# A graph layer with a routed feed-forward stage: three last tiles kept out of the sums, their rows gathered and matched in pairs, and the copy to the output in chunks of five rows

## The chip, the cores and the metric

One core of a Trainium2 chip runs the kernel. The metric is the time of the device in microseconds (us) of one execution. TensorE (PE in the profile, its weight loads PEld) multiplies matrices, VectorE (DVE) and ScalarE (ACT) work on elements, GpSimd (POOL) issues the indirect DMAs, SyncE (SP) and ScalarE issue the plain ones. All DMAs of the core run on its 16 DMA engines.

## What is computed

The input is x (1250 x 768) with a graph of 41250 edges. The kernel computes two graph attention layers and a linear attention, adds them to x, and then a routed feed-forward stage. Only this last stage matters here:

```python
gate = xt @ Wg + bg
scores, idx = jax.lax.top_k(gate, TOP_K)          # TOP_K = 2 of 8 experts
h = jax.nn.gelu(jnp.einsum('td,edh->eth', xt, W1) + b1[:, None, :], approximate=False)
y = jnp.einsum('eth,ehd->etd', h, W2) + b2[:, None, :]
comb = jnp.sum(jax.nn.one_hot(idx, NUM_EXPERTS, dtype=x.dtype) * scores[..., None], axis=1)
out = jnp.einsum('te,etd->td', comb, y)
x = x + out
```

So each row of the output is the row of x plus two weighted rows, one from each expert that was chosen for it.

## The kernel before, in words

The rows are sorted by expert into NTL = 27 tiles of 128 places. A tile holds rows of one expert only; places that are left over point at a row past the end (N = 1250 rows, NP = 1280). A row of x has two places, in two different tiles, because its two experts differ. `found[:, i]` holds, for each of the 128 places of tile i, the number of its row. `acc_d` in DRAM starts as x, and the weighted rows are added to it.

For each tile i, the following happens:

- Pool gathers the tile's normalized rows from `xf_d` into the buffer `XR[:, i % 3]` (`rows_gather`, line 863), three tiles ahead.
- TensorE turns them (`rows_in`, line 2183), ScalarE copies them out of PSUM (line 1113), TensorE multiplies by the first weights (`up`, products of line 1783 and a bias product of line 2192), ScalarE takes the Gelu (line 1118, for the last tile line 1121), TensorE turns the result (`turn`, line 2199), VectorE splits it into two fp16 parts (`HT`, lines 1756 and 1757), TensorE multiplies by the second weights (`down`, line 1783 and the bias product of line 2209), and VectorE scales the result by the score into `Yb[:, i % 2]` (line 1773).
- Pool adds `Yb` to the rows of `acc_d` by an indirect DMA that accumulates (`sums_add`, line 870). Each addition waits until the one before it has landed, since two tiles can hold the same row.

TensorE's order in the loop is: rows_in(i + 1), turn(i - 1), up(i), down(i - 1); behind the loop come turn(26), a product for shared rows, and down(26). VectorE's order is HT(i), then Yb(i). Each engine works through its own list in order, so what stands behind a waiting instruction waits too.

The last two tiles are not added to `acc_d`. LATE = NTL - 2 = 25 is the first of them. When the additions of tiles 0 to 24 have landed, `acc_d` is copied to `out`, rows 0 to 639 from SP's queue (line 749) and the other 610 from ACT's (line 1124), both as one contiguous block. At the same time Pool gathers the rows of tiles 25 and 26 from `acc_d` into XR (line 887). VectorE adds `Yb` of tile 25 to the first (line 1761). A row may stand in both tiles. The matrix `same` (128 x 128, one where place k of tile 25 and place n of tile 26 hold the same row) is made before the loop: TensorE spreads `foundf` of one tile over all partitions (line 2219), VectorE compares it with the other's (line 1745) and reduces it to a flag for each place (line 1747). A product of `same` with `Yb` of tile 25 (line 2238) is added to tile 26's rows (line 1765), and with its own result that gives the final rows (line 1770). Two scatters write them to `out` (lines 891 and 894), once both copies are complete; a place of tile 25 whose row stands in tile 26 too is skipped, because its number in `lasti` is made larger than N.

Of the kernel before, what the change touches and what calls it, by code (L numbers as in the profile page):

```python
# [15 lines left out]
P = 128  # L16
# [7 lines left out]
def gps_layer(nc, x, src, dst, norm_g, norm_b, W1, a_src1, a_dst1, b1, W2, a_src2, a_dst2, b2, Wu, bu,  # L24
# [27 lines left out]
    with ctx:  # L52
# [157 lines left out]
        def low(off, words, rows=P):  # L210
            return arena[0:rows, LOW + off:LOW + off + words]
# [67 lines left out]
        same = low(5 * D + MAPW, P)  # L279
        shared, lastf = low(5 * D + MAPW + P, 1), low(5 * D + MAPW + P + 1, 1)  # L280
        lasti = low(5 * D + MAPW + P + 2, 1).bitcast(I32)
        assert P + 3 <= MAPW
# [255 lines left out]
        LATE = NTL - 2  # L538
# [17 lines left out]
        def _(sp):  # L556
# [192 lines left out]
            sp.dma_start(out[0:NT // 2 * P, :], acc_d[0:NT // 2 * P, :]).then_inc(s_out_done, 16)  # L749
# [5 lines left out]
        def _(pool):  # L755
# [134 lines left out]
            pool.wait_ge(s_y_ready, NTL)  # L890
            g.indirect_dma_start(out=out, out_offset=bass.IndirectOffsetOnAxis(ap=lasti.bitcast(U32), axis=0), in_=XR[:, (LATE - 1) % 3, :], in_offset=None,
                                 bounds_check=N - 1, oob_is_err=False).then_inc(sums_out[LATE % 2], 16)
            pool.wait_ge(s_y_ready, NTL + 1)
            g.indirect_dma_start(out=out, out_offset=bass.IndirectOffsetOnAxis(ap=found[:, NTL - 1:NTL].bitcast(U32), axis=0), in_=Yb[:, (NTL - 1) % 2, :], in_offset=None,
                                 bounds_check=N - 1, oob_is_err=False).then_inc(sums_out[(NTL - 1) % 2], 16)
# [3 lines left out]
        def _(act):  # L899
# [209 lines left out]
            for i in range(NTL):  # L1109
# [16 lines left out]
        @block.vector  # L1126
        def _(dve):
# [620 lines left out]
            link(V.scalar_tensor_tensor(lastf, shared, float(4 * NP), foundf[:, LATE:LATE + 1], ALU.mult, ALU.add))  # L1748
            link(V.tensor_copy(lasti, lastf))

            for i in range(NTL):
# [6 lines left out]
                if i == NTL - 1:  # L1758
                    dve.wait_ge(s_y_ready, LATE + 1)
                    dve.wait_ge(rows_back[(LATE - 1) % 3], 16 * ((LATE - 1) // 3 + 2))  # L1760
                    V.tensor_tensor(XR[:, (LATE - 1) % 3, :], XR[:, (LATE - 1) % 3, :], Yb[:, LATE % 2, :], ALU.add).then_inc(s_y_ready, 1)
                    dve.wait_ge(s_same_psum, 1)
                    dve.wait_ge(rows_back[LATE % 3], 16 * (LATE // 3 + 2))
                    before = XR[:, LATE % 3, :].rearrange("p (a n) -> p a n", a=2)
                    link(V.tensor_tensor(before, PS[:, 0:1024].rearrange("p (a n) -> p a n", a=2)[:, :, 0:HALF], before, ALU.add))
                dve.wait_ge(s_y_psum, i + 1)
                if i >= 2:
                    dve.wait_ge(sums_out[i % 2], 16 * (i // 2))
                if i == NTL - 1:
                    V.scalar_tensor_tensor(Yb[:, i % 2, :].rearrange("p (a n) -> p a n", a=2), PS[:, 5 * 512:7 * 512].rearrange("p (a n) -> p a n", a=2)[:, :, 0:HALF],  # L1770
                                           score[:, 1, i:i + 1], before, ALU.mult, ALU.add).then_inc(s_y_ready, 1)
                    break
                V.tensor_scalar(Yb[:, i % 2, :].rearrange("p (a n) -> p a n", a=2), PS[:, 5 * 512:7 * 512].rearrange("p (a n) -> p a n", a=2)[:, :, 0:HALF], score[:, 1, i:i + 1], None, ALU.mult).then_inc(s_y_ready, 1)  # L1773

        @block.tensor
        def _(pe):
# [442 lines left out]
            T.matmul(ps[7][:, 0:P], foundf[:, NTL - 1:NTL].to_broadcast([P, P]), ident[:, :], start=True, stop=True).then_inc(s_map_psum, 1)  # L2219
# [15 lines left out]
            pe.wait_ge(s_y_ready, LATE + 1)  # L2235
# [31 lines left out]
```

## Time and profile before

| what | us |
|---|---|
| median of three runs | 1122.6 (1119.86 to 1125.56) |
| the profiled execution, its own time | 1124.17 |
| its span | 1122.4 |
| TensorE busy | 979.9 (87%) |
| VectorE busy | 763.9 (68%) |
| ScalarE busy | 332.1 (30%) |
| GpSimd busy | 117.8 (10%) |

Times within the trace are counted from the start of the span. "Busy" says that an engine had an instruction at work, not that it set the time. PEclk is the granted clock of TensorE as a share of full speed.
### The profile page before, as it was taken

How to read it: one execution, taken by the hardware profiler on the slowest of the kernel's cores; microseconds unless marked ns; L12 is line 12 of the kernel's file. 1: busy time of each engine (PE TensorE's matmuls, PEld its weight loads, DVE VectorE, ACT ScalarE, POOL GpSimd, SP SyncE). 2: the span in 40 equal slices, each digit the busy share in tenths (PEclk: the TensorE clock that was granted, in tenths of full speed). 3: DMA queues.
4: the chain of work that ended last, by engine and by line, in shares of the span. 5: the costliest groups of instructions: out<-in, count | busy, mean ns of one | idle time of the engine just before them, and what ended most of it. 6: DMA issues, size and time to landing. Idle time of an engine off the chain costs nothing.

```text
span 1122.4 us, 17272 instructions
## 1 busy us (share of the span) xinstructions
PE 979.9 (87%) x6464; PEld 707.8 (63%) x6466; DVE 763.9 (68%) x1711; ACT 332.1 (30%) x402; POOL 117.8 (10%) x125
## 2 busy tenths in 40 slices
PE   3699999999789989989988998959878399999992
PEld 2677776765454445546678998759765366666661
DVE  6576788878875686986587898499979823222321
ACT  3551122212004331422333343115335332222220
POOL 3000000000001000000000000000631123333321
PEclk9799999999989999999989999868898589999997
DMA  8341121144240926636686100006046545555535
GB/s 243 123 143 44 44 84 58 57 153 158 103 180 29 314 98 207 204 103 231 221 328 288 47 1 1 1 0 254 5 170 231 208 102 109 113 113 104 103 63 179
DMA packets 58570, 146.45 MB, mean 130 GB/s; under 512 B 11562, under 2 KB 30908, under 8 KB 55482
## 3 DMA queue, kind: packets, MB, share of 16 engines
q1 hardware_dynamic: 49482, 114.37, 28.9%
q0 software_dynamic: 6080, 21.24, 9.3%
q10 hardware_dynamic: 2928, 9.74, 2.3%
q8 instruction: 54, 0.88, 0.3%
q14 instruction: 26, 0.21, 0.1%
HBM read 96.73 MB, written 53.23 MB: 134 GB/s over the span
## 4 chain that ended last, share of the span: by engine, by line
PE 64%; DVE 21%; DMA 6%; issue 4%; ACT 3%; SPq 1%; DVEq 0%; POOLq 0%; ACTq 0%
PE PS L1783 37%; PE PS L2032 12%; PE PS L1859 3%; DVE arena L1522 3%; DVE arena L1478 2%; DVE arena L1484 2%; PE PS L2183 2%; DMA arena<-in_L_ffn_W_dram 1%; DMA arena<-acc_d,arena 1%; PE PS L1870 1%; DMA acc_d<-arena 1%; PE PS L1839 1%; PE PS L1874 1%; DVE arena L1494 1%; DVE arena L1384 1%
## 5 line engine op out<-in xcount | busy, mean ns | idle before, releaser
L1783 PE MATMUL PS<-arena 128*128 128x384 f16 (+7 forms) x3396 | 575.6, 323 | 5.5 <-DVE arena L1638 2.7
L1783 PEld LDWEIGHTS PS<-arena 128*128 128x128 f16 (+2 forms) x3396 | 321.6, 99 | 217.5 <-issue 12.8
L2032 PE MATMUL PS<-arena 128*128 128x193 f32 (+1 forms) x1200 | 190.5, 322 | 21.9 <-DVE arena L1484 16.6
L2032 PEld LDWEIGHTS PS<-arena 128*128 128x128 f32 x1200 | 186.0, 200 | 26.4 <-DVE arena L1484 16.1
L1046 ACT ACTIVATE arena<-arena,AS 128x1280 f32<-128x1280 f32 x60 | 81.8, 1363 | 132.4 <-DVE arena L1478 132.2
L1773 DVE TENSOR_SCALAR arena<-PS,arena 128x768 f32<-128x768 f32 x26 | 26.5, 1018 | 134.5 <-PE PS L2209 134.5
L1478 DVE SCALAR_TENSOR_TENSOR arena<-arena,AS 128x1280 f32<-128x1280 f32 x60 | 94.1, 1572 | 0.0
L1484 DVE SCALAR_TENSOR_TENSOR arena<-arena 128x1280 f32<-128x1280 f32 x60 | 90.5, 1508 | 3.5 <-PE PS L2032 3.5
L1286 DVE TENSOR_SCALAR arena<-arena 128x240 f16<-128x240 f16 x324 | 89.4, 276 | 0.0
L1285 DVE TENSOR_SCALAR arena<-arena 128x128 f16<-128x128 f16 x324 | 80.5, 248 | 0.1
L1113 ACT ACTIVATE arena<-PS 128x1536 f16<-128x1536 f16 x27 | 39.2, 1450 | 100.1 <-PE PS L2183 100.1
L1384 DVE CUSTOM_DVE_ANT_0 arena<-arena 128x1280 bf16<-128x1280 f32 x40 | 59.5, 1489 | 2.4 <-DMA arena<-as_d 1.6
L1859 PE MATMUL PS<-arena 128*128 128x240 f16 x324 | 44.8, 270 | 12.9 <-DVE arena L1278 12.9
L940 ACT ACTIVATE arena<-arena 128x768 f16<-128x768 f32 x48 | 39.8, 838 | 53.5 <-DMA arena<-in_L_ffn_W_dram 53.4
L1239 DVE SCALAR_TENSOR_TENSOR arena<-arena 128x768 f16<-128x768 f32 x48 | 45.5, 954 | 13.1 <-ACT arena L940 12.6
L870 POOL DMA_INDIRECT acc_d<-arena x25 | 39.7, 1586 | 118.6 <-DVE arena L1773 118.6
L1859 PEld LDWEIGHTS PS<-arena 128*128 128x128 f16 x324 | 31.1, 98 | 24.9 <-DVE arena L1286 15.6
L1278 DVE TENSOR_TENSOR arena<-arena,PS 128x240 f32 x81 | 32.4, 400 | 12.8 <-PE PS L1859 11.4
L863 POOL DMA_INDIRECT arena<-xf_d,arena x27 | 26.7, 988 | 63.8 <-DVE arena L1721 49.0
L1522 DVE CUSTOM_DVE_ANT_0 arena<-PS,arena 128x1280 bf16<-128x1280 f32 x20 | 28.4, 1485 | 5.4 <-PE PS L2048 5.4
L793 POOL MEMSET arena<- 128x768 bf16 x1 | 0.7, 743 | 288.3 <-DMA bias_d<-arena 288.3
L972 ACT ACTIVATE arena<-PS 128x384 f32<-128x384 f32 x20 | 8.7, 488 | 70.7 <-PE PS L1783 70.7
(289 smaller groups left out, 961.5 us busy)
## 6 DMA issues: line engine op xcount, KB each, us to landing
arena<-in_L_ffn_W_dram SPq DMA_DIRECT2D x48, 384.0 KB, 4.0
fr_d<-arena SPq DMA_DIRECT2D x48, 384.0 KB, 3.2
arena<-fr_d SPq DMA_DIRECT2D x16, 1152.0 KB, 14.4
arena<-in_x_dram SPq DMA_DIRECT2D x18, 384.0 KB, 5.3
arena<-rr_d SPq DMA_DIRECT2D x4, 1280.0 KB, 8.6
acc_d<-arena SPq DMA_DIRECT2D x11, 384.0 KB, 2.6
g_d<-arena SPq DMA_DIRECT2D x10, 388.0 KB, 2.4
acc_d<-arena ACTq DMA_DIRECT2D x10, 384.0 KB, 2.4
```

Of the source, the lines that this page charges most:

```text
L940: a.activation(cbuf[b][:, PIECE:PIECE + PIECE // 2].bitcast(F16), cbuf[b][:, 0:PIECE], ACT.Copy, scale=UP).then_inc(s_conv_high, 1)
L1046: a.activation(BUF[:, unit % 3, :], BUF[:, unit % 3, :], ACT.Exp, bias=AS2[:, h, t:t + 1]).then_inc(s_e_ready, 1)
L1239: V.scalar_tensor_tensor(buf[:, 0:PIECE // 2].bitcast(F16), buf[:, 0:PIECE], UP, buf[:, PIECE:PIECE + PIECE // 2].bitcast(F16), ALU.mult, ...
L1285: V.tensor_scalar(ohlo[:, u % OB, j, :], iota[:, 0:P], kc[:, 1, j, u:u + 1], None, ALU.is_equal)
L1286: i = V.tensor_scalar(ohk[:, u % OB, j, :], iota[:, 0:NT * W], kc[:, 0, j, u:u + 1], None, ALU.is_equal)
L1384: V.tensor_tensor_reduce(out=junk1, in0=arow1[h], in1=mask1[d % 2].rearrange("p t d -> p (t d)"), scale=1.0, scalar=-3e38, op0=ALU.subtrac ...
L1478: V.scalar_tensor_tensor(BUF[:, unit % 3, :], RR[:, h % 2, 0, :], AS8[:, h, t:t + 1], RR[:, h % 2, 1, :], ALU.add, ALU.max).then_inc(s_t2_ ...
L1484: V.scalar_tensor_tensor(PT[i % deep], BUF[:, unit % 3, :], 2.0, CT[:, t, 0:NP], ALU.min, ALU.mult).then_inc(s_p_ready, 1)
L1522: V.tensor_tensor_reduce(out=junk2[:, n % 2, :], in0=PS[:, bank:bank + NP], in1=mask2[:, t, :], scale=1.0, scalar=-3e38, op0=ALU.subtract, ...
L1783: m = T.matmul(out, left[i][x], right[i][y], start=first and i + r == 0, stop=last and 3 * i + r == n - 1)
L1859: i = T.matmul(ps[4 + u % 2][:, 0:NT * W], ohlo[:, u % OB, j, :], ohk[:, u % OB, j, :], start=j == 0, stop=j == EJ - 1)
L2032: m = T.matmul(ps[b][:, r * (C + 1):(r + 1) * (C + 1)], PT[i % deep][:, d * P:(d + 1) * P], feats, start=t == 0 and r == 0, stop=t == NT - ...
```

## The change

LATE becomes NTL - 3 = 24, so tiles 24, 25 and 26 are kept out of the sums. Their rows are gathered from `acc_d`, each tile into the XR buffer that its own rows have left. A row can now stand in two of the three tiles, in three ways, so `same` becomes three matrices (24 in 25, 24 in 26, 25 in 26), and TensorE makes three products behind turn(26) instead of one. `shared` and `lasti` have two columns. VectorE adds Yb(24) to tile 24's gathered rows directly behind Yb(24) in its order. The copy of `acc_d` to `out` is cut at row 650 instead of 640, and both parts are named as ten times 13 (or 12) chunks of five rows of 3072 bytes, with the ten outermost. ACT's copy now stands ahead of its last Gelu. Three scatters follow the copies instead of two. The core of the diff:

```diff
-        LATE = NTL - 2
+        LATE = NTL - 3
+        CUT = 650
@@ SP
-            sp.dma_start(out[0:NT // 2 * P, :], acc_d[0:NT // 2 * P, :]).then_inc(s_out_done, 16)
+            sp.dma_start(out[0:CUT, :].rearrange("(a b r) n -> b a (r n)", b=10, r=5), acc_d[0:CUT, :].rearrange("(a b r) n -> b a (r n)", b=10, r=5)).then_inc(s_out_done, 16)
@@ Pool
             for i in range(LATE, NTL):
-                b = (i - 1) % 3
-                pool.wait_ge(s_xrt_psum, i)
+                b = i % 3
+                pool.wait_ge(s_xrt_psum, i + 1)
                 g.indirect_dma_start(out=XR[:, b, :], out_offset=None, in_=acc_d,
...
+            for i in range(LATE, NTL):
+                pool.wait_ge(s_y_ready, (LATE + 2, LATE + 4, LATE + 5)[i - LATE])
+                last = i == NTL - 1
+                g.indirect_dma_start(out=out, out_offset=bass.IndirectOffsetOnAxis(ap=(found[:, i:i + 1] if last else lasti[:, i - LATE:i - LATE + 1]).bitcast(U32), axis=0),
+                                     in_=Yb[:, i % 2, :] if last else XR[:, i % 3, :], in_offset=None,
+                                     bounds_check=N - 1, oob_is_err=False).then_inc(sums_out[i % 2], 16)
@@ ScalarE, in the tile loop
+                if i == NTL - 1:
+                    for b in range(2):
+                        act.wait_ge(sums_out[b], added(b, LATE))
+                    a.dma_start(out[CUT:N, :].rearrange("(a b r) n -> b a (r n)", b=10, r=5), acc_d[CUT:N, :].rearrange("(a b r) n -> b a (r n)", b=10, r=5)).then_inc(s_out_done, 16)
...
-            for b in range(2):
-                act.wait_ge(sums_out[b], added(b, LATE))
-            a.dma_start(out[NT // 2 * P:N, :], acc_d[NT // 2 * P:N, :]).then_inc(s_out_done, 16)
@@ VectorE, before the tile loop
-            V.tensor_scalar(same, ps[7][:, 0:P], foundf[:, LATE:LATE + 1], None, ALU.is_equal).then_inc(s_found_ready, 1)
+            for k, (a, b) in enumerate(((0, 1), (0, 2), (1, 2))):
+                j = V.tensor_scalar(same[:, k, :], ps[7][:, (b - 1) * P:b * P], foundf[:, LATE + a:LATE + a + 1], None, ALU.is_equal)
...
-            link(V.tensor_reduce(shared, same, axis=AX.X, op=ALU.max))
+            V.tensor_reduce(shared[:, 0:1], same[:, 0:2, :].rearrange("p k n -> p (k n)"), axis=AX.X, op=ALU.max)
+            link(V.tensor_reduce(shared[:, 1:2], same[:, 2, :], axis=AX.X, op=ALU.max))
+            def rows_read(i):
+                dve.wait_ge(rows_back[i % 3], 16 * (i // 3 + 2))
+
+            def shared_add(i, banks):
+                for c in range(2):
+                    h = rows_of(i)[:, c * HALF:(c + 1) * HALF]
+                    k = V.tensor_tensor(h, h, ps[banks[c]][:, 0:HALF], ALU.add)
+                link(k)
@@ VectorE, behind HT(NTL - 1)
+                    rows_read(LATE + 1)
                     dve.wait_ge(s_same_psum, 1)
+                    shared_add(LATE + 1, (0, 1))
+                    V.tensor_tensor(rows_of(LATE + 1), rows_of(LATE + 1), Yb[:, (LATE + 1) % 2, :], ALU.add).then_inc(s_y_ready, 1)
+                    rows_read(LATE + 2)
+                    dve.wait_ge(s_same_psum, 2)
+                    shared_add(LATE + 2, (7, 3))
@@ VectorE, behind Yb(i)
+                if i == LATE:
+                    dve.wait_ge(s_y_ready, LATE + 1)
+                    rows_read(LATE)
+                    V.tensor_tensor(rows_of(LATE), rows_of(LATE), Yb[:, LATE % 2, :], ALU.add).then_inc(s_y_ready, 1)
+                elif i == LATE + 1:
+                    dve.wait_ge(s_y_ready, LATE + 3)
@@ TensorE
-                    pe.wait_ge(s_y_ready, i)
+                    pe.wait_ge(s_y_ready, i + max(0, i - LATE - 1))
...
-            T.matmul(ps[7][:, 0:P], foundf[:, NTL - 1:NTL].to_broadcast([P, P]), ident[:, :], start=True, stop=True).then_inc(s_map_psum, 1)
+            for b in range(2):
+                m = T.matmul(ps[7][:, b * P:(b + 1) * P], foundf[:, LATE + 1 + b:LATE + 2 + b].to_broadcast([P, P]), ident[:, :], start=True, stop=True, skip_group_check=True)
+            m.then_inc(s_map_psum, 1)
...
-            for c in range(2):
-                m = T.matmul(ps[c][:, 0:HALF], same, Yb[:, LATE % 2, c * HALF:(c + 1) * HALF], start=True, stop=True)
-            m.then_inc(s_same_psum, 1)
+            def shared_part(k, y, banks, first, last):
+                for c in range(2):
+                    m = T.matmul(ps[banks[c]][:, 0:HALF], same[:, k, :], Yb[:, y % 2, c * HALF:(c + 1) * HALF], start=first, stop=last)
+                return m
+
+            shared_part(0, LATE, (0, 1), True, True).then_inc(s_same_psum, 1)
+            shared_part(1, LATE, (7, 3), True, False)
+            pe.wait_ge(s_y_ready, LATE + 3)
+            shared_part(2, LATE + 1, (7, 3), False, True).then_inc(s_same_psum, 1)
             down(NTL - 1, before)
```

## Rows read from the trace of the kernel before

**Rows 1.** The chain that ended last, 1080 to 1123 us: start, us, what

```profile
1084.53 7.09 DMA acc_d<-arena
...
1092.34 5.37 DMA acc_d<-arena
...
1097.98 14.69 DMA arena<-acc_d,arena
```

**Rows 2.** Timeline, 1060 to 1123: start, us, engine, line, what [idle before <-releaser]

```profile
1093.64 0.33 PE L2192 MATMUL PS<-arena 104*128 104x384 bf16 x1
...
1094.00 0.49 ACT L1121 ACTIVATE arena<-PS 128x384 f32<-128x384 f32 x1 [6.19 <-PE PS L2192]
...
1097.06 0.49 PE L2199 MATMUL PS<-ident,arena 128*128 128x128 f32 x3
1097.26 1.02 DVE L1773 TENSOR_SCALAR arena<-PS,arena 128x768 f32<-128x768 f32 x1 [4.60 <-PE PS L2209]
1097.73 0.61 SPq L749 DMA_DIRECT2D out_dram<-acc_d  x1
...
1098.34 1.56 PE L2238 MATMUL PS<-arena 128*128 128x384 f32 x4 [0.78 <-DVE arena L1773]
1098.78 0.56 DVE L1757 TENSOR_TENSOR arena<-PS,arena 128x384 f16<-128x384 f32 x1
1099.30 0.98 POOL L887 DMA_INDIRECT arena<-acc_d,arena  x1 [0.31 <-issue]
...
1099.73 1.63 PE L1783 MATMUL PS<-arena 128*128 x9
...
1102.82 0.33 PE L2209 MATMUL PS<-arena 104*128 104x384 bf16 x1
1112.76 0.96 DVE L1761 TENSOR_TENSOR arena<-arena 128x768 f32<-128x768 f32 x1 [13.42 <-DMA arena<-acc_d,arena]
...
1114.68 1.02 DVE L1770 SCALAR_TENSOR_TENSOR arena<-PS,arena 128x768 f32<-128x768 f32 x1
1116.53 1.01 POOL L894 DMA_INDIRECT out_dram<-arena  x1 [0.87 <-DVE arena L1770]
```

**Rows 3.** DMA queues, stretches 1099:1101.7, 1101.7:1104.35, 1104.35:1105.4: packets, MB, share

```profile
q1 hardware_dynamic: 16, 0.98, 102.1%
...
q10 hardware_dynamic: 16, 0.94, 96.7%
...
q1 hardware_dynamic: 16, 0.98, 282.7%
q0 software_dynamic: 16, 0.10, 28.5%
```

**Rows 4.** Timeline at the start of the tile loop, 885 to 918

```profile
902.08 0.80 PE L2219 MATMUL PS<-ident,arena 128*128 128x128 f32 x2
...
907.83 0.56 DVE L1756 CAST arena<-PS 128x384 f16<-128x384 f32 x1 [3.78 <-PE PS L2199]
```

**Rows 5.** DMA view of 1084 to 1092, in 40 slices of 0.2 us

```profile
GB/s 0 0 0 0 0 0 0 0 0 0 0 0 0 230 15 108 154 108 138 61 61 200 215 200 215 123 108 97 15 0 0 0 0 0 0 0 0 0 0 0
```

**Rows 6.** DMA queues, 576 to 581, loads of 1152 KB: packets, MB, share

```profile
q1 hardware_dynamic: 133, 2.02, 96.4%
```

**Rows 7.** DMA view, 788 to 793: six loads of eight rows

```profile
DMA packets 97, 0.12 MB, mean 24 GB/s; under 512 B 48, under 2 KB 72, under 8 KB 96
```

**Rows 8.** Line 863, the row gathers of the tile loop

```profile
DMA to landing us min/median/max: 4.0/5.1/5.9
```

**Rows 9.** Stretches (start:end us): busy us (instructions) of each engine, PEclk, DMA, GB/s

```profile
309.00:316.60 7.60, 6.74 (x24) 3.40 (x25) 3.40 (x18) 0.00 (x0) 0.00 (x0) 0.50 1.02 378
572.60:576.04 3.44, 3.42 (x11) 3.44 (x12) 3.44 (x3) 1.36 (x1) 0.12 (x1) 0.50 0.51 148
1103.20:1108.50 5.30, 0.00 (x0) 0.00 (x0) 0.00 (x0) 0.00 (x0) 0.00 (x0) 1.00 1.16 370
1108.50:1112.00 3.50, 0.00 (x0) 0.00 (x0) 0.00 (x0) 0.00 (x0) 0.00 (x0) 0.50 0.38 134
```

More of the change, by code:

```diff
@@ L278, in gps_layer @@
         foundf = low(5 * D, NTL)
[L279 to L282, printed above, removed]
+        same = v3(low(5 * D + MAPW, 3 * P), 3)
+        shared, lastf = (low(5 * D + MAPW + 3 * P + 2 * k, 2) for k in range(2))
+        lasti = low(5 * D + MAPW + 3 * P + 4, 2).bitcast(I32)
+        assert MAPW + 3 * P + 6 <= D
         found = small(NTL).bitcast(I32)
@@ L536, in copies_of @@
             return range(s - 4, s - 3) if s < NT + 2 else range(2 * s - NT - 6, 2 * s - NT - 4)
-        LATE = NTL - 2
+        LATE = NTL - 3
+        CUT = 650
+        assert CUT < N and CUT % 50 == 0 and (N - CUT) % 50 == 0
         def added(b, n):
@@ L889, in _ @@
             pool.wait_ge(s_out_done, 32)
[L890 to L895, printed above, removed]
+            for i in range(LATE, NTL):
[4 more added lines that the diff above has]
+                                     bounds_check=N - 1, oob_is_err=False).then_inc(sums_out[i % 2], 16)
         @block.scalar
@@ L1744, in _, with rows_of @@
             dve.wait_ge(s_map_psum, 3)
-            V.tensor_scalar(same, ps[7][:, 0:P], foundf[:, LATE:LATE + 1], None, ALU.is_equal).then_inc(s_found_ready, 1)
+            for k, (a, b) in enumerate(((0, 1), (0, 2), (1, 2))):
+                j = V.tensor_scalar(same[:, k, :], ps[7][:, (b - 1) * P:b * P], foundf[:, LATE + a:LATE + a + 1], None, ALU.is_equal)
+            j.then_inc(s_found_ready, 1)
             dve.wait_ge(s_found_ready, 3)
-            link(V.tensor_reduce(shared, same, axis=AX.X, op=ALU.max))
-            link(V.scalar_tensor_tensor(lastf, shared, float(4 * NP), foundf[:, LATE:LATE + 1], ALU.mult, ALU.add))
+            V.tensor_reduce(shared[:, 0:1], same[:, 0:2, :].rearrange("p k n -> p (k n)"), axis=AX.X, op=ALU.max)
+            link(V.tensor_reduce(shared[:, 1:2], same[:, 2, :], axis=AX.X, op=ALU.max))
+            link(V.scalar_tensor_tensor(lastf, shared, float(4 * NP), foundf[:, LATE:LATE + 2], ALU.mult, ALU.add))
             link(V.tensor_copy(lasti, lastf))
+            def rows_of(i):
+                return XR[:, i % 3, :]
+            def rows_read(i):
[5 more added lines that the diff above has]
+                link(k)
             for i in range(NTL):
@@ L1758, in _ @@
                 if i == NTL - 1:
-                    dve.wait_ge(s_y_ready, LATE + 1)
-                    dve.wait_ge(rows_back[(LATE - 1) % 3], 16 * ((LATE - 1) // 3 + 2))
-                    V.tensor_tensor(XR[:, (LATE - 1) % 3, :], XR[:, (LATE - 1) % 3, :], Yb[:, LATE % 2, :], ALU.add).then_inc(s_y_ready, 1)
+                    rows_read(LATE + 1)
                     dve.wait_ge(s_same_psum, 1)
-                    dve.wait_ge(rows_back[LATE % 3], 16 * (LATE // 3 + 2))
-                    before = XR[:, LATE % 3, :].rearrange("p (a n) -> p a n", a=2)
-                    link(V.tensor_tensor(before, PS[:, 0:1024].rearrange("p (a n) -> p a n", a=2)[:, :, 0:HALF], before, ALU.add))
+                    shared_add(LATE + 1, (0, 1))
[3 more added lines that the diff above has]
+                    shared_add(LATE + 2, (7, 3))
                 dve.wait_ge(s_y_psum, i + 1)
                 if i >= 2:
-                    dve.wait_ge(sums_out[i % 2], 16 * (i // 2))
+                    dve.wait_ge(sums_out[i % 2], 16 * (min(i, LATE) // 2 if i % 2 == 0 else min(i // 2, LATE // 2)))
                 if i == NTL - 1:
+                    dve.wait_ge(s_same_psum, 2)
+                if i == NTL - 1:
+                    before = rows_of(i).rearrange("p (a n) -> p a n", a=2)
                     V.scalar_tensor_tensor(Yb[:, i % 2, :].rearrange("p (a n) -> p a n", a=2), PS[:, 5 * 512:7 * 512].rearrange("p (a n) -> p a n", a=2)[:, :, 0:HALF],
```

1 line of the change is left out of this document (removed).

## The prediction, made before the change was run

> **What bounds the kernel now.** I read the chain that ended last first, then the timeline of the last 60 us, then the DMA view of the same stretch in short slices. The tile loop is bound by TensorE up to tile 26, the last. The end is bound by transfers. The chain [rows 1] shows the addition of tile 23's rows to acc_d (issued at 1084.53, landed 7.09 us later, at 1091.6), that of tile 24 (issued at 1092.34, landed at 1097.71), and then 14.69 us for the gather of tile 25's rows back from acc_d, to 1112.67. TensorE has finished long before: its last matmul begins at 1102.82 and takes 0.33, so it ends at 1103.15 [rows 2]. Then VectorE runs from 1112.76 to 1115.70, and the last scatter is issued at 1116.53 [rows 2]. So the two gathers and the two copies of acc_d to out, all issued from 1097.73 to 1099.30 [rows 2], set the end.
>
> Why does a gather take 14.7 us, when the loop's gathers land 5.1 us after their issue [rows 8]? The three slices of the DMA view [rows 3] show it. From 1099 to 1101.7 there are 16 packets of SP's queue and nothing else, from 1101.7 to 1104.35 16 of ACT's queue, and then 16 of the gathers' (q0) before the next 16 of SP's. Each of the 16 DMA engines thus takes one packet of each queue in turn. A copy's packet is 0.98 MB / 16 = 61 KB and takes 102.1% x 16 x 2.7 us / 16 = 2.76 us (22 KB/us); a gather's is 0.10 MB / 16 = 6 KB, two rows, and takes 28.5% x 1.05 us = 0.30 us. A gather of 128 rows has four of them per engine, then an end marker.
>
> **The change, part by part.** I follow tile 24's rows, which after the change are gathered, and no longer added to acc_d.
>
> 1. Start of the copies. They now wait for tile 23's sum alone, landed at 1091.6 instead of 1097.71: 6.1 us earlier [rows 1]. SP's queue is otherwise empty. On ACT the copy now stands ahead of the last Gelu, which starts at 1094.00 [rows 2]; the issue begins at about 1091.7 and takes about the 0.61 us of SP's [rows 2], so 1.7 us of slack cover it. Without that cover the Gelu would be late by as much, but turn(26), which reads it, comes only after the new wait of step 3. Pool's gathers go from two to three, each 1.3 us after the one before (0.98 and 0.31 idle [rows 2]): at about 1091.9, 1093.2 and 1094.5.
>
> 2. Landing of gather 24. Its first data move about 2.1 us after the issue (tile 23's sum: issued at 1084.53, first slice with data at 1086.6 [rows 1, 5]), so at 1094.0. The copies' first packets start 1.4 us after the issue (issued at 1097.73, and all 16 of SP's first packets lie in the slice that begins at 1099 and fill it, [rows 2, 3]), so at 1093.05. Their chunks are five rows, 15.4 KB. No row before shows such a copy between two DRAM tensors. The lower bound is a load of packets of 15 KB, 96.4% x 16 x 5 / 133 = 0.58 us [rows 6]; the upper one is 0.75 us, the rate of the later 61 KB packets (282.7% x 1.05 = 2.97 us [rows 3]). I take 0.69, from 2.76 us for 61 KB, the same kind of transfer at its first, less mixed packets. One turn is 0.69 + 0.69 + 0.27 = 1.65 us. The first gather packet goes at 1093.05 + 2 x 0.69 = 1094.4, the marker four turns on at 1101.0, and the gather lands at 1101.2. The bounds are 1097.0 (5.1 us after the issue, [rows 8]) and 1103.3 (0.9 us a packet, if small packets carry a cost of their own).
>
> 3. What waits for it. VectorE's add for tile 24 is put between Yb(24) and the HT copies of tile 25. So the wait for the gather now stands ahead of those copies, and TensorE's down(25) waits for them. In the kernel before these went on at 1098. TensorE ends up(26) at 1093.97 [rows 2] and idles. From the landing on, everything runs in series: the add 0.96 (1.05 with its start), HT(25) 1.1 (from 1098.28 to 1099.34), down(25) 3.8 (1099.34 to 1103.15), turn(26) 0.5, three shared parts of 1.4 each (L2238: 1098.34 to 1099.73 for one, and there are now three) 4.2, down(26) 3.4 (1099.73 to 1103.15), and the last VectorE instruction 1.05: in sum 15.1 us [rows 2]. HT(26), and the new adds for tiles 25 and 26 (five instructions of 0.56 to 1.0), run beside the shared parts and down(26), and Yb(25) ends before part three needs it. That gives 1101.2 + 15.1 = 1116.3 as the end of VectorE, against 1115.70 before.
>
> 4. The clock. TensorE idles from 1093.97 to about 1103.4, 9.4 us. Before, it had the full granted clock for 5.3 us of idling and half of it (1.2 instead of 2.4 GHz) from 1108.5 on [rows 9]. So down(25) starts at half. When work came back after such gaps, the clock stayed at half for 3.4 us in one case (572.60 to 576.04) and 7.6 us in another (309.00 to 316.60) [rows 9]. The mean is 5.5 us, and half of it is lost: 2.7 us (1.7 to 3.8). VectorE then ends at 1119.0, or 3.3 us later than before.
>
> 5. Setup of the matches. Two fp32 products stand before the loop instead of one. One shows as two records, 0.80 us in all [rows 4]; TensorE starts the loop right behind them, so the second costs at most 0.8 and, since the two are pipelined, about 0.3. The added VectorE work (two comparisons, a wider reduction) is under 1.5 us and lies inside the 3.78 us that VectorE idles before its first HT copy [rows 4]. I take 0.3.
>
> 6. The transfers' own end. Each of the six loads of eight rows left eight end markers (48 packets under 512 B [rows 7]): a queue's transfer uses as many engines as its outer count allows. With an outer count of ten the copies run on ten engines, 13 and 12 chunks on each: 1093.05 + 25 x 0.69 + 12 x 0.27 = 1113.5, about as late as before in spite of the earlier start. The other two gathers end within a us of that. Pool then issues three scatters at 1.3 us each: the third could go at 1116.4, while step 4 asks for 1119.8. So the transfers are late second, not first.
>
> The sum: 3.3 + 0.3 = +3.6 us. The profiled execution took 1124.17 with a span of 1122.4, and would become 1127.8; it lies 1.6 above the median of the three runs, so the median becomes 1122.6 + 3.6 = 1126.2.
>
> **The rivals.**
>
> - Gather 24 lands unhindered, at 1097.0, and TensorE's gap of 5.3 us doesn't lower the clock. VectorE would end at 1112.1, but the transfers hold: with 0.58 us a packet the copies end at 1110.7, the last gather at about 1111.3, and its two VectorE instructions at 1113.4. That is 2.3 less, 0.3 more for the setup: -2.0, 1120.6. For it: q0 is served in turn and its packets are short. Against it: in rows 3 the turns are strict.
> - The copies' packets cost 0.9 us, and the ten engines decide. Gather 24 lands at 1103.3, the copies end at 1093.05 + 22.5 + 3.2 = 1118.8 and the third scatter goes at 1121.7 instead of 1116.53: +5.2 + 0.3, 1128.1. It decides from about 0.85 us a packet.
> - Slower still: a queue's turn holds several chunks. If it held all 13, gather 24 would wait for both copies: 1093.05 + 25 x 0.69 + 4 x 0.27 + 0.2 = 1111.6, 10.4 later than in the forecast, 1136.6. Against it: the loads of rows 6 leave one packet per 15 KB row. The Trainium skill (DMA: Bandwidth & Descriptors, Queues, rings and completion order) says that an engine drains a whole packet, typically 9 to 17 descriptors, from one ring before it goes to the next; by that rule this rival is the forecast. The trace doesn't show such packets on SP's queue.
> - The clock stays at half to the end of the chain: the 11.5 us of TensorE's work in step 3 double. Above the 2.7 taken that is +8.8, 1135.0. Against it: the chain keeps TensorE busy after its resumption, and in both cases of rows 9 the clock came back.
>
> **How the numbers follow.** The forecast 0.60, unhindered 0.12, ten engines 0.12, several chunks a turn 0.08, half clock 0.08. Within 0.5% (5.6 us, about what a measurement of this kernel can tell from no change) lie nearly all of the first two and half of the third: 0.70. Slower by more are the last two, the other half of the third and a tail of the first: 0.25. To be faster by 5.6 us VectorE would have to end at 1110.1, earlier than gather 24's lower bound allows: 0.05. The range takes in the unhindered case with 2 us to spare and ten engines with 3: 1118.5 to 1131.5, leaving out the two at 1135 and later.
>
> **What would show it.** In the profile after: two HT copies of tile 25 that start near 1102 with a wait of some 10 us before the VectorE add; TensorE idle for about 9 us after up(26), a granted clock of 0.5 behind that; 25 packets of 15 KB on ten engines only; the last VectorE instruction at about 1119. The prediction is wrong if gather 24 lands before 1099 or after 1104, if the clock holds, or if the last scatter waits for the copies.

## The result and the profile after

The changed kernel takes 1127.9 us (median of seven runs) against 1122.6: a ratio of 1.0045, with a 95% interval of 1.003 to 1.006. Timed once more beside the kernel before, it came out at 1.0022 (1.0003 to 1.0041). So it is slower by a quarter to a half of a percent, 2.5 to 5 us. The forecast was +3.6 us, 1126.2. The profiled execution has a span of 1126.1 us; the forecast was 1126.0. That agreement to 0.1 us is luck: a second profile of the same kernel has a span of 1123.6.

The chain that ended last in the changed kernel, 1080 to 1127 us (start, us, what):

```profile
1092.24 10.94 DMA arena<-acc_d,arena
...
1104.73 0.57 DVE arena L1775
...
1105.43 3.06 PE PS L1810 x9
...
1111.11 3.87 PE PS L2268 x12
```

One gather sets it off, as in [rows 1], but it takes 10.94 us and is followed by TensorE's work, which in the kernel before was over by then. The timeline shows the same stretch (start, us, engine, line, what, idle before and its releaser):

```profile
1091.53 0.89 SPq L751 DMA_DIRECT2D out_dram<-acc_d  x1
1091.54 1.71 ACTq L1124 DMA_DIRECT2D out_dram<-acc_d  x1
1091.69 1.02 DVE L1794 TENSOR_SCALAR arena<-PS,arena 128x768 f32<-128x768 f32 x1 [5.20 <-PE PS L2236]
...
1092.24 1.02 POOL L889 DMA_INDIRECT arena<-acc_d,arena  x1 [5.05 <-issue]
...
1094.75 0.33 PE L2219 MATMUL PS<-arena 104*128 104x384 bf16 x1
...
1095.11 0.49 ACT L1127 ACTIVATE arena<-PS 128x384 f32<-128x384 f32 x1 [6.19 <-PE PS L2219]
1103.27 0.96 DVE L1798 TENSOR_TENSOR arena<-arena 128x768 f32<-128x768 f32 x1 [10.56 <-DMA arena<-acc_d,arena]
...
1105.43 3.06 PE L1810 MATMUL PS<-arena 128*128 x9 [10.36 <-DVE arena L1775]
...
1110.94 4.04 PE L2268 MATMUL PS<-arena 128*128 128x384 f32 x12
...
1118.34 1.02 DVE L1791 SCALAR_TENSOR_TENSOR arena<-PS,arena 128x768 f32<-128x768 f32 x1 [2.23 <-issue]
1120.15 0.98 POOL L895 DMA_INDIRECT out_dram<-arena  x1 [3.38 <-DVE arena L1791]
```

Up(26) ends at 1095.08. VectorE waits 10.56 us for the gather of tile 24, the two HT copies of tile 25 stand behind that wait (the second ends at 1105.29), and TensorE idles for 10.36 us. All else follows in series up to 1119.36. In [rows 2] up(26) ended at 1093.97 and down(25) followed at once.

The granted clock over the gap and behind it (start:end, length, busy us with the count of instructions for PE, PEld, DVE, ACT, POOL, then PEclk, DMA share, GB/s):

```profile
1095.10:1099.00 3.90, 0.00 (x0) 0.00 (x0) 0.00 (x0) 0.49 (x1) 0.70 (x1) 1.00 0.93 364
1099.00:1105.40 6.40, 0.00 (x0) 0.00 (x0) 1.98 (x3) 0.00 (x0) 0.00 (x0) 0.51 0.63 267
1105.43:1109.40 3.97, 3.97 (x13) 1.97 (x14) 0.00 (x0) 0.00 (x0) 0.00 (x0) 0.50 0.62 261
1109.40:1114.00 4.60, 4.60 (x22) 2.92 (x20) 3.08 (x6) 0.00 (x0) 1.02 (x1) 1.00 0.19 81
```

And the DMA queues over the copies (1092.8 to 1112.3), one turn of the engines (1103.6 to 1105), the stretch in which the copies begin (1092.8 to 1095.4), and the slice with the first packets of ACT's queue (1096.4 to 1096.6): packets, MB, share.

```profile
q1 hardware_dynamic: 140, 2.00, 25.3%
q10 hardware_dynamic: 130, 1.84, 22.3%
q0 software_dynamic: 240, 1.18, 15.9%
...
q1 hardware_dynamic: 10, 0.15, 25.6%
q10 hardware_dynamic: 10, 0.15, 25.6%
q0 software_dynamic: 10, 0.06, 10.4%
...
q1 hardware_dynamic: 34, 0.52, 57.0%
...
q10 hardware_dynamic: 5, 0.08, 104.0%
```

In the first three rows, 130 and 120 chunks of 15.4 KB are counted, with ten end markers for each of the two copies. One turn, 1103.6 to 1105, holds ten packets of each queue: ten engines, on each one packet of SP, one of ACT, one of the gathers. 25.6% x 16 x 1.4 / 10 = 0.573 us is a chunk's time, 0.233 a gather packet's. From 1092.8 to 1095.4 only SP's queue moves anything, 34 chunks: neither ACT's copy, issued at 1091.54, nor the first gather, issued at 1092.24, had begun. The gathers' first packets come at 1095.4, 3.2 us behind the issue, and ACT's at 1096.4, 4.9 us behind its own. So the turns of one packet for each queue are there later, but not at the start.

**How the runs are compared.** The part ahead of the tail varies from one execution to the next: Yb(24), the scaling of tile 24 on VectorE, starts anywhere from 1085.9 to 1093.9 us in the profiles of this study, though nothing ahead of it differs but the setup of the matches. So each profile is also read from the start of Yb(24) to the end of the span. It is called the tail below. Part of the tail still varies by chance: the sum of tile 23, behind which the copies and gathers of the changed kernels start, lands anywhere from 0.4 us before Yb(24)'s start to 1.1 us after it. So the table also gives the time from that landing to the end (SP issues its copy 0.06 us behind the landing, and that is where the landing is read in the kernels with three late tiles). The profiles are single executions; only the ratios come with an interval.

| kernel | Yb(24) starts | span | tail | from tile 23's landing | ratio to before (95%) |
|---|---|---|---|---|---|
| before | 1090.59 | 1122.4 | 31.8 | 30.8 | |
| changed | 1091.69 | 1126.1 | 34.4 | 34.6 | 1.0045 (1.003 to 1.006) |
| e13_changed_again | 1088.90 | 1123.6 | 34.7 | 34.5 | 1.0022 (1.0003 to 1.0041) |
| e1_add_later | 1090.69 | 1119.5 | 28.8 | 29.2 | 0.9977 (0.9958 to 0.9996) |
| e2_add_later_16 | 1088.49 | 1115.4 | 26.9 | 27.0 | 0.9970 (0.9948 to 0.9992) |
| e11_add_later_whole | 1089.16 | 1117.1 | 27.9 | 27.6 | 0.9949 (0.9925 to 0.9973) |
| e9_two_rows_16 | 1093.89 | 1120.2 | 26.3 | 26.1 | 0.9931 (0.9908 to 0.9954) |
| e12_two_rows_again | 1089.70 | 1115.8 | 26.1 | 26.3 | 0.9944 (0.9919 to 0.9969) |
| e4_sixteen | 1090.41 | 1128.2 | 37.8 | 36.7 | 1.0048 (1.0025 to 1.0072) |
| e3_whole_copies | 1091.59 | 1129.5 | 37.9 | 38.1 | 1.0063 (1.0040 to 1.0086) |
| e8_before_16 | 1085.94 | 1118.0 | 32.1 | 31.1 | 0.9993 (0.9972 to 1.0014) |
| e5_no_copies | 1087.81 | 1115.9 | 28.1 | 27.2 | one execution |
| e6_filler | 1090.70 | 1124.9 | 34.2 | 34.5 | one execution |
| e10_filler_60 | 1089.73 | 1122.4 | 32.7 | 33.1 | one execution |

### The profile page after: what moved, and what is told of

Read it like the earlier page. It is cut to its first block and busy times, and to the rows that moved or that the text cites. A ratio compares the mean times of both kernels' runs of the same rounds, so it can differ in the third digit from the quotient of the medians.

```text
span 1126.1 us, 17301 instructions
## 1 busy us (share of the span) xinstructions
PE 985.7 (88%) x6474; PEld 713.3 (63%) x6476; DVE 767.7 (68%) x1718; ACT 332.6 (30%) x402; POOL 118.3 (11%) x126
## 5 line engine op out<-in xcount | busy, mean ns | idle before, releaser
L2059 PE MATMUL PS<-arena 128*128 128x193 f32 (+1 forms) x1200 | 193.4, 325 | 21.9 <-DVE arena L1487 16.5
L2059 PEld LDWEIGHTS PS<-arena 128*128 128x128 f32 x1200 | 188.9, 202 | 26.3 <-DVE arena L1487 16.0
L872 POOL DMA_INDIRECT acc_d<-arena x24 | 38.1, 1588 | 112.4 <-DVE arena L1794 112.4
```

The source lines that it names most:

```text
L2059: m = T.matmul(ps[b][:, r * (C + 1):(r + 1) * (C + 1)], PT[i % deep][:, d * P:(d + 1) * P], feats, start=t == 0 and r == 0, stop=t == NT - ...
```

## The experiments

Theory A is the forecast's: VectorE's wait for gather 24 stands ahead of the HT copies of tile 25, TensorE stops, and the serial chain behind the landing sets the end. Theory B is the rival that the transfers set it, with the copies on ten engines.

### The add moved behind HT(26)

```diff
@@ VectorE, behind HT(NTL - 1)
+                    dve.wait_ge(s_y_ready, LATE + 2)
+                    rows_read(LATE)
+                    V.tensor_tensor(rows_of(LATE), rows_of(LATE), Yb[:, LATE % 2, :], ALU.add).then_inc(s_y_ready, 1)
                     rows_read(LATE + 1)
@@ VectorE, behind Yb(i)
-                if i == LATE:
-                    dve.wait_ge(s_y_ready, LATE + 1)
-                    rows_read(LATE)
-                    V.tensor_tensor(rows_of(LATE), rows_of(LATE), Yb[:, LATE % 2, :], ALU.add).then_inc(s_y_ready, 1)
-                elif i == LATE + 1:
-                    dve.wait_ge(s_y_ready, LATE + 3)
```

The counts that TensorE and Pool wait for are changed to match.

> The changed kernel with VectorE's add for tile 24 moved behind HT(26), so that no HT copy stands behind the wait for gather 24. Theory A (the wait in VectorE's order stops TensorE, and the serial chain behind it sets the end): TensorE no longer idles for 10 us, down(26) ends at 1095.1 + 3.3 + 0.5 + 4.2 + 3.4 = 1106.5, then the transfers decide: last gather 1112.1, two VectorE instructions of 1.0, end of VectorE 1114.2 instead of 1119.4, so about -5 us against the changed kernel: 1122.8, level with the kernel before. Theory B (the copies on ten engines set the end): nothing moves, 1127.9 within 1 us.

The timeline of e1_add_later:

```profile
1093.91 1.63 PE L1807 MATMUL PS<-arena 128*128 x9
...
1102.35 0.96 DVE L1779 TENSOR_TENSOR arena<-arena 128x768 f32<-128x768 f32 x1 [2.90 <-DMA arena<-acc_d,arena]
...
1104.46 0.33 PE L2233 MATMUL PS<-arena 104*128 104x384 bf16 x1
1108.42 1.02 DVE L1766 TENSOR_TENSOR arena<-arena,PS 128x384 f32<-128x384 f32 x2 [5.12 <-DMA arena<-acc_d,arena]
...
1111.56 1.02 DVE L1794 SCALAR_TENSOR_TENSOR arena<-PS,arena 128x768 f32<-128x768 f32 x1
...
1113.51 0.98 POOL L895 DMA_INDIRECT out_dram<-arena  x1 [0.31 <-issue]
```

TensorE goes on at once (1093.91) and ends at 1104.79, with the last matmul's record at 1104.46. The wait for gather 24 is still there, 2.90 us in front of the add at 1102.35, and costs nothing. What is late now is gather 25 (5.12 us of waiting before 1108.42), gather 26 and the copies, after which the three scatters go out 1.3 us apart, the last at 1113.51. The tail fell from 34.4 to 28.8, by 5.6 us where A expected 5 and B nothing. The ratio fell from 1.0045 to 0.9977; A had expected only to come level with the kernel before. One moved wait is the whole of the loss and more: A holds. B is right about what comes second, as step 6 had it.

### The copies on 16 engines, with the add moved and without

```diff
-            sp.dma_start(out[0:CUT, :].rearrange("(a b r) n -> b a (r n)", b=10, r=5), acc_d[0:CUT, :].rearrange("(a b r) n -> b a (r n)", b=10, r=5)).then_inc(s_out_done, 16)
+            sp.dma_start(out[0:640, :].rearrange("(a b r) n -> b a (r n)", b=16, r=5), acc_d[0:640, :].rearrange("(a b r) n -> b a (r n)", b=16, r=5)).then_inc(s_out_done, 16)
+            sp.dma_start(out[1200:N, :].rearrange("(a b r) n -> b a (r n)", b=10, r=5), acc_d[1200:N, :].rearrange("(a b r) n -> b a (r n)", b=10, r=5)).then_inc(s_out_done, 16)
```

ACT copies rows 640 to 1199 in the same way. e2_add_later_16 has this and the moved add, e4_sixteen this alone.

> As e1_add_later, and the copies with 16 outermost instead of ten (rows 0 to 639 and 640 to 1199 in chunks of five rows, the last 50 rows apart). Theory A: both limits move. Copies 15 packets of 0.57 and 12 gather packets of 0.23 on each engine, 11.4 us from 1093.2 on, so the last gather lands near 1106, TensorE ends near 1106.5, VectorE near 1108: -11 us against the changed kernel, 1116.5, about 0.5% faster than before. Theory B expects the gain of the copies alone: about -5.

> The changed kernel with only the copies spread over 16 engines, the chunks still five rows, VectorE's order untouched. Theory A: a gather packet still waits for one packet of each copy queue in every turn, gather 24 lands at about 1103 as before, and the chain behind it is unchanged: 1127.9 within 1.5. Theory B: copies end near 1106 instead of 1111.6: -5 us, 1123.

The gathers and the last VectorE instruction in e2_add_later_16, then the wait for gather 24 in e4_sixteen:

```profile
1088.43 0.65 SPq L751 DMA_DIRECT2D out_dram<-acc_d  x1
...
1102.30 0.96 DVE L1780 TENSOR_TENSOR arena<-arena 128x768 f32<-128x768 f32 x1 [5.06 <-DMA arena<-acc_d,arena]
1104.63 1.02 DVE L1767 TENSOR_TENSOR arena<-arena,PS 128x384 f32<-128x384 f32 x2 [1.36 <-DMA arena<-acc_d,arena]
...
1107.60 1.02 DVE L1795 SCALAR_TENSOR_TENSOR arena<-PS,arena 128x768 f32<-128x768 f32 x1
1109.42 0.98 POOL L896 DMA_INDIRECT out_dram<-arena  x1 [0.94 <-DVE arena L1795]
...
1105.33 0.96 DVE L1799 TENSOR_TENSOR arena<-arena 128x768 f32<-128x768 f32 x1 [13.89 <-DMA arena<-acc_d,arena]
```

With the add moved, the 16 engines bring the tail down to 26.9, 7.5 us less than in the changed kernel where 11 had been expected. The direction is A's; the size was wrong in two places. Gather 25 landed 16.2 us behind SP's issue and gather 26 about 17, where 14.5 had been expected for the last, because I added packet times as if 16 engines ran at the pace of ten: in e4_sixteen, over 1092.5 to 1107, SP's queue has a share of 43.2% of 14.5 us for 138 chunks, 0.73 us each, where the same reading gave 0.61 on ten. And VectorE ended 4.0 us behind gather 25's landing, where 2 had been allowed behind the last gather's.

Without the moved add, 16 engines gained nothing, as A said, and B's -5 us did not come. But gather 24 did not land as before, as A had it: it took 12.92 us from its issue instead of 10.94. The add waited 13.89 us instead of 10.56, and the tail grew by 3.4, to 37.8. Of that, 1.4 us is chance: in this execution the sum of tile 23 landed 1.1 us behind the start of Yb(24), in the changed kernel's 0.2 us before it. Counted from the landing the end is 2.0 us later, as much as gather 24 is. The ratio, 1.0048, can't be told from the changed kernel's. In this order, then, ten engines did no harm: their copies end at 1111.6, 7.8 us before VectorE, so their slower end costs nothing, and gather 24 comes 2.0 us sooner.

### The whole copies

e3_whole_copies is the changed kernel with the contiguous halves of the kernel before, e11_add_later_whole that with the moved add.

```diff
-            sp.dma_start(out[0:CUT, :].rearrange("(a b r) n -> b a (r n)", b=10, r=5), acc_d[0:CUT, :].rearrange("(a b r) n -> b a (r n)", b=10, r=5)).then_inc(s_out_done, 16)
+            sp.dma_start(out[0:NT // 2 * P, :], acc_d[0:NT // 2 * P, :]).then_inc(s_out_done, 16)
```

> The changed kernel with the copies of the kernel before (contiguous halves, packets of 61 and 58 KB on 16 engines). Theory A: gather 24 has to sit through both packets of each copy queue on every engine and lands at about 1106.3 instead of 1103.2, the chain starts 3 us later: 1131. Theory B: the copies end 5 us earlier than with ten engines, 1123.

> The changed kernel with VectorE's add moved as in e1_add_later, and the whole, contiguous copies of the kernel before. If chunks matter only through the number of engines: transfers end some 17 us after the copies' issue as with five-row chunks on 16 engines, and the end of the span is 27 us behind Yb(24)'s start, as in e2_add_later_16. If small packets help by themselves, it is 2 us or more later than that.

The VectorE add that waits for gather 24, in the one and in the other, then gather 24 from issue to landing in e4_sixteen and in e3_whole_copies (start, us, what):

```profile
1106.79 0.96 DVE L1798 TENSOR_TENSOR arena<-arena 128x768 f32<-128x768 f32 x1 [14.19 <-DMA arena<-acc_d,arena]
...
1105.43 0.96 DVE L1779 TENSOR_TENSOR arena<-arena 128x768 f32<-128x768 f32 x1 [7.52 <-DMA arena<-acc_d,arena]
...
1092.32 12.92 DMA arena<-acc_d,arena
...
1092.16 14.54 DMA arena<-acc_d,arena
```

In e3_whole_copies the add starts at 1106.79, 3.5 us later than in the changed kernel, and the tail is longer by 3.5. The edit undoes two things at once, the chunks and the ten engines, and e4_sixteen stands between them. From issue to landing, gather 24 took 10.94 us with five-row chunks on ten engines, 12.92 with the same chunks on 16, and 14.54 with whole halves on 16. So in these profiles 2.0 us of the 3.6 go with the ten engines and 1.6 with the chunks. Both matter because a chain hangs on this landing. B expected a gain from the 16 engines and none came. With the add moved, the same late landing costs little: tail 27.9, 1.0 more than with chunks on 16 engines, 0.9 less than with chunks on ten. There gathers land together and late, and five VectorE instructions and the final one follow in series.

### The copies nearly left out

e5_no_copies copies 16 rows on each queue instead of 650 and 600. Most rows of its output are never written.

```diff
-            sp.dma_start(out[0:CUT, :].rearrange(...), acc_d[0:CUT, :].rearrange(...)).then_inc(s_out_done, 16)
+            sp.dma_start(out[0:16, :], acc_d[0:16, :]).then_inc(s_out_done, 16)
```

> The changed kernel with the two copies of acc_d to out cut down to 16 rows each, so most rows of the output are never written. It prices the contention. Theory A: gather 24 lands about 5 us after its issue instead of 10.9, TensorE idles for some 5 us instead of 10.4, and the chain behind the landing keeps its length of about 15 to 16 us: end of VectorE 5 to 6 us earlier against Yb(24) than in the changed kernel. Theory B (transfers) expects gather 24 and the end to move by the same amount too; the two differ in what is left: by A the end is still 15 to 16 us behind gather 24's landing though no transfer is under way any more, by B VectorE ends right behind the last gather, at about 1100.

```profile
1089.46 1.02 POOL L889 DMA_INDIRECT arena<-acc_d,arena  x1 [6.15 <-issue]
...
1093.43 0.96 DVE L1798 TENSOR_TENSOR arena<-arena 128x768 f32<-128x768 f32 x1 [4.59 <-DMA arena<-acc_d,arena]
...
1108.10 1.02 DVE L1791 SCALAR_TENSOR_TENSOR arena<-PS,arena 128x768 f32<-128x768 f32 x1 [2.23 <-issue]
```

In the DMA view, from 1090.4 to 1090.8 and from 1090.8 to 1091.2:

```profile
q10 hardware_dynamic: 32, 0.05, 42.1%
...
q0 software_dynamic: 4, 0.02, 47.1%
```

Gather 24 landed 3.9 us after its issue, where A expected 5, so the copies cost it 7 us. Part of that is a late start. Here ACT's copy, issued at 1088.76, moves its data between 1090.4 and 1090.8, and the gathers begin between 1090.8 and 1091.2, under 2 us behind the issue of 1089.46. In the changed kernel the same two waited 4.9 and 3.2 us. So the late start there goes with SP's large copy under way, and is no fixed delay of the two queues; by what mechanism no run shows. The last VectorE instruction still ends 15.8 us behind the landing (1093.33 to 1109.12), with no copy or gather under way for the last 12. That is A, and B is out: with the transfers gone, the chain alone gives a tail of 28.1 us, more than e2_add_later_16 has with full copies. VectorE's end came 6.4 us earlier against Yb(24) than in the changed kernel, where 5 to 6 had been expected.

### The clock

Matmuls whose result nobody reads fill TensorE's gap.

```diff
                 up(i, e)
+                if i == NTL - 1:
+                    for _ in range(48):
+                        T.matmul(ps[7][:, 0:HALF], identh[:, :], XRTP[:, 0, 0, 0:3, :].rearrange("p k n -> p (k n)"), start=True, stop=True)
                 if i:
                     down(i - 1, before)
```

> The changed kernel with 48 matmuls of 384 columns, whose result nobody reads, between up(26) and down(25), about 7.8 us of TensorE work in the gap. Theory of the clock: the granted clock stays at full, down(25) takes 3.4 instead of 5.35 us, and the chain from gather 24's landing to the end of VectorE shrinks from 16.2 to about 14.3 us. If the clock had no part in it, the chain stays at 16.2.

> As e6_filler, but 60 matmuls instead of 48, 9.9 us, so that no more than about 0.6 us of idling is left ahead of down(25) (with 48, TensorE idled for 2.55 us and the granted clock was at half for 3.4 us all the same). If the clock has its part in the chain, it stays at full and the chain from gather 24's landing to the end of VectorE takes about 14.3 us instead of 16.2. If not, it stays near 16.

The stretches of e6_filler (48) and then of e10_filler_60 (60), columns as above:

```profile
1101.88:1104.43 2.55, 0.00 (x1) 0.00 (x1) 1.98 (x3) 0.00 (x0) 0.00 (x0) 1.00 0.65 277
...
1105.00:1108.40 3.40, 3.40 (x13) 1.54 (x12) 0.00 (x0) 0.00 (x0) 0.00 (x0) 0.50 0.57 236
...
1102.86:1103.60 0.74, 0.00 (x1) 0.00 (x1) 0.57 (x2) 0.00 (x0) 0.00 (x0) 1.00 0.68 291
1103.61:1107.00 3.39, 3.39 (x22) 2.16 (x23) 0.00 (x0) 0.00 (x0) 0.00 (x0) 1.00 0.63 261
```

With 48, the filler ended 2.55 us before down(25) could start, and the clock still went to half from 1105.0 to 1108.4: a miss, and no answer to the question (its chain took 16.0 us). With 60, the gap was 0.74 us and the clock held. The chain from the landing (1101.36) to the end of VectorE (1115.62) then took 14.3 us, as expected, against 16.2 in the changed kernel (1103.18 to 1119.36). The clock's part is 1.9 us, and the tail fell by 1.7, to 32.7. Each of the two is one execution.

### The kernel before with chunked copies

e8_before_16 is the kernel before with only its copies changed, in the chunks of e2_add_later_16.

```diff
-            sp.dma_start(out[0:NT // 2 * P, :], acc_d[0:NT // 2 * P, :]).then_inc(s_out_done, 16)
+            sp.dma_start(out[0:640, :].rearrange("(a b r) n -> b a (r n)", b=16, r=5), acc_d[0:640, :].rearrange("(a b r) n -> b a (r n)", b=16, r=5)).then_inc(s_out_done, 16)
```

> The kernel before (two late tiles) with only its copies changed: chunks of five rows on 16 engines, the last 50 rows apart. Theory A, by which small packets by themselves give nothing once the copies and the gathers end together: the last gather lands within 1 us of before, 1122.7 within 1.5. If small packets free the gathers: both land some 2 to 3 us earlier, 1120.

0.9993 (0.9972 to 1.0014), tail 32.1 against 31.8: nothing. Where copies and gathers all have to be in before the end, the size of the copies' packets didn't matter here.

### Chunks of two rows

e9_two_rows_16 is e2_add_later_16 with r=2 and the last 34 rows as one block on SP's queue; e12_two_rows_again is the same kernel.

```diff
-            sp.dma_start(out[0:640, :].rearrange("(a b r) n -> b a (r n)", b=16, r=5), ...)
-            sp.dma_start(out[1200:N, :].rearrange("(a b r) n -> b a (r n)", b=10, r=5), ...)
+            sp.dma_start(out[0:640, :].rearrange("(a b r) n -> b a (r n)", b=16, r=2), ...)
+            sp.dma_start(out[1216:N, :], acc_d[1216:N, :]).then_inc(s_out_done, 16)
```

> As e2_add_later_16, but with chunks of two rows (6 KB) instead of five, the last 34 rows as one block. A turn of an engine costs 0.23 x 3 = 0.7 us instead of 1.4, so the gathers come through before the copies end: gather 26 lands before the copies, VectorE ends near TensorE, and the third scatter follows the copies' end by 0.3 + 2.6: about 2 us less against Yb(24) than e2_add_later_16 (26.9 from there to the end of the span, so 25). If small packets cost more per byte, the copies end later and nothing is gained.

> The kernel of e9_two_rows_16 once more, timed beside e11_add_later_whole and the kernel before: about 0.5 to 0.7% faster than before, and 26 to 27 us from Yb(24)'s start to the end of the span. If the first measurement was a chance of the chip, it is level with e2_add_later_16, 0.3% faster.

The first five lines are of e12_two_rows_again, with its first scatter among them, the last is the add for tile 24 in e9_two_rows_16:

```profile
1099.57 0.96 DVE L1780 TENSOR_TENSOR arena<-arena 128x768 f32<-128x768 f32 x1 [1.12 <-DMA arena<-acc_d,arena]
...
1106.18 1.02 DVE L1767 TENSOR_TENSOR arena<-arena,PS 128x384 f32<-128x384 f32 x2 [0.34 <-DMA arena<-acc_d,arena]
1107.24 1.02 DVE L1795 SCALAR_TENSOR_TENSOR arena<-PS,arena 128x768 f32<-128x768 f32 x1
1107.24 1.02 POOL L896 DMA_INDIRECT out_dram<-arena  x1 [13.43 <-DMA out_dram<-acc_d]
...
1109.88 0.98 POOL L896 DMA_INDIRECT out_dram<-arena  x1 [0.30 <-issue]
...
1104.84 0.96 DVE L1780 TENSOR_TENSOR arena<-arena 128x768 f32<-128x768 f32 x1 [2.19 <-DMA arena<-acc_d,arena]
```

The add for tile 24 starts 9.9 us behind the start of Yb(24) in e12_two_rows_again and 11.0 in e9_two_rows_16, where it was 11.7 in e1_add_later and 13.8 in e2_add_later_16, and the three gathers now come one after the other. The first scatter follows the copies' end, and the other two follow it without a gap, the last 1.6 us behind VectorE's end at 1108.26. The tails are 26.3 and 26.1 where 25 had been expected: the copies ended 15.8 and 16.1 us behind their issue, against 15.1 with five rows in e2_add_later_16, which takes back 0.7 to 1.0 of the 2 us. Against e2 the two-row chunks gain 0.6 to 0.8 us of tail, which the ratios can't resolve. Against the kernel before, 0.9931 and 0.9944 are clear: this kernel, three late tiles with the add behind HT(26), is about 0.6% faster than the kernel before and about 1% faster than the changed one.

### The changed kernel once more

> The changed kernel itself once more. In its first profile the end of the span was 34.4 us behind the start of Yb(24), against 31.8 before, so the changed part accounts for +2.6 us, while the medians differ by 5.3. If the rest lies in the part ahead of Yb(24), which the change doesn't touch, and is a matter of the runs, the ratio comes out nearer to 1.0025 and the tail again near 34.4. If the tail itself varies and the first profile had a short one, the tail comes out at 36 to 37 and the ratio near 1.0045.

The tail was 34.7 and the ratio 1.0022: the first of the two. The changed part accounts for +2.6 and +2.9 us of tail in the two profiles. Counted from the landing of tile 23's sum it is +3.8 and +3.7: in the profile before that sum took 7.09 us to land, in these two 5.8 and 6.2, which makes their tails look shorter. The rest of the first timing's +5.3 isn't explained by anything behind the landing; the two intervals meet at 1.003 to 1.0041, and I take +3.4 to +4.6 us as what both allow.

## Why the prediction was right, step by step

The size came out right, but in part because two misses cancel each other. Counted from the landing of tile 23's sum (1091.6 before, 1091.47 after):

- **Step 1, start of the copies: right.** SP issued at 1091.53 and ACT at 1091.54. ACT's issue took 1.71 us instead of the 0.61 assumed; its Gelu started at 1095.11, so the cover held, and it held with 1.9 us left. The gathers followed at 1092.24, 1093.57 and 1094.85, the first 0.8 us behind the landing and not 0.3.
- **Step 2, landing of gather 24: the turns right, the start wrong.** Forecast 9.6 us behind the sum, measured 11.7 (1103.18). Strict turns of one packet for each queue are there, and on ten engines, but only once all three queues move. A turn cost 1.4 us, not 1.65, since a chunk took 0.573 us, the lower bound of [rows 6] and not the 0.69 that I took from the 61 KB packets. The start was the error: I let gather data begin 2.1 us after the issue [rows 5] and take turns with both copies from then on, and nothing of q0 moved before 1095.4, 3.2 us after it, while SP's queue alone moved 34 chunks. Four turns of 1.4 us back from the end marker, 0.2 us ahead of the landing, the first gather packet on the ten shared engines came at about 1097.4 (an estimate), some 3 us later than my 1094.4. The shorter turns give 1.0 back, and +2.1 us is left. e5_no_copies shows that the 2.1 us were not too short for a gather without large copies beside it.
- **Step 3, the serial chain: right, 0.8 us too long.** 14.3 us at full clock (e10_filler_60) against 15.1. The add and the first HT copy overlap by 0.1, and the three shared parts took 3.9 us to the next matmul and not 4.2.
- **Step 4, the clock: right, 0.8 us too large.** It was at half from 1099 to 1109.4, 4.0 us of them behind down(25)'s start, and cost 1.9 us, inside the bounds of 1.7 to 3.8. Its two cases in [rows 9], 3.4 and 7.6 us, were averaged to 5.5; the shorter was nearer. The second miss, 1.6 us in steps 3 and 4 together, stands against the 2.1 of step 2.
- **Step 5, the setup: right.** The two products began at 903.29 and the loop's first at 904.30, 1.0 us after it where it was 0.9 before: 0.1 instead of 0.3. VectorE idled 2.40 us ahead of its first HT copy instead of 3.78.
- **Step 6, the transfers second: right.** Copies ended at 1111.6, forecast 1113.5; the first scatter went at 1112.46 and the third waited 3.38 us for VectorE, not for the copies. e1_add_later shows them take over once the chain is gone.

Of the rivals, the unhindered gather fell in step 2: it was e5_no_copies that had it, at the price of no copies. Ten engines as the bound, several chunks a turn, and a clock at half to the end didn't occur. (The last has a slip: TensorE's work in step 3 adds up to 11.9 us, not 11.5, and the rival to 1135.4; nothing else hangs on it.) The rule of the Trainium skill (DMA: Bandwidth & Descriptors, Queues, rings and completion order) by which a turn holds 9 to 17 descriptors would have put the landing at 1111.6; the landing was at 1103.18, and the turns of the profile after hold one 15 KB chunk of each queue. Before the other queues moved, SP's sent over three chunks an engine.

What the prediction did not look for is that the +3.6 us were avoidable: it priced the wait where it stood. The diff already shows that the add for tile 24 writes rows that only the first scatter reads, so HT(25), Yb(25) and HT(26) can all go ahead of it.

## What to carry to other kernels

- When work is taken out of a DMA queue and given to a compute engine, find what stands behind its wait in that engine's order before looking at the transfer. Here one wait placed ahead of two copies turned a gain of 3.0 us of tail into a loss of 2.6 (1.6 and 3.8 counted from the landing of tile 23's sum); placed five instructions later it cost nothing.
- Chunking a large copy brings a small transfer that shares its engines forward: 1.6 us for gather 24 with five-row chunks on 16 engines. That is worth time where something hangs on the first of them. Where all must be in before the end, it gave nothing in the kernel before (e8_before_16) and 1.0 us of tail, or 0.6 counted from the landing, with the add moved (e2_add_later_16 against e11_add_later_whole), too little for the ratios to show.
- An edit that changes the chunks and the number of engines together needs a run that changes one of them. Here the number of engines had the larger part.
- In a kernel whose front part varies by several us from one execution to the next, read a change in the tail from a fixed event and not from the span, and take the event that releases the changed part: counted from Yb(24), e4_sixteen looked 1.4 us worse than it was.

## What the runs showed of the hardware

- Beside a large copy that SP had just issued, ACT's queue and the gathers began late. In the changed kernel ACT's first packets came 4.9 us behind its issue and the gathers' 3.2 us behind theirs, where SP's own came 1.6 us behind; only SP's packets moved until 1095.4. With the copies nearly left out (e5_no_copies) ACT's came under 2 us behind its issue, and so did the gathers'. In the kernel before this can't be seen, since SP's first 61 KB packets cover the time [rows 3].
- Behind an idle gap of 2.55 us on TensorE the granted clock was at half for 3.4 us (e6_filler), behind one of 0.74 us it stayed full (e10_filler_60).
- A chunk of 15 KB from DRAM to DRAM took 0.573 us in one turn of ten engines. Over the whole copy it was 0.61 on SP's queue with ten engines at work and 0.73 with 16 (e4_sixteen), so 16 engines carried the copies and three gathers in about 17 us where ten took 20, not in ten sixteenths of it.
- The issue of a copy took longer with ten outermost: 0.89 us on SP and 1.71 on ACT in the changed kernel, 0.65 and 0.68 with 16 outermost (e2_add_later_16), 0.61 and 0.62 for the whole copies of the kernel before.
